# Cross attention in half chunks of 128 steps and groups of eight heads, with the queries in two slots

## The chip, the cores and the metric

The kernel runs on one core of a Trainium2 chip. The metric is the device time of one execution in microseconds (us); lower is better. Engines: PE is TensorE (matmul), PEld its weight loads, DVE VectorE, ACT ScalarE, POOL GpSimd, SP the queue that issues nearly all DMAs.

## What is computed

A two-layer decoder on x[2, 1024, 256] with a context of 77 rows. Layer 0 is self attention, cross attention and a mixture of eight linear experts; layer 1 is a tanh recurrence over the 1024 steps, cross attention and a gated mixture of experts. Each sublayer reads a layer norm of x and is added to x. Cut to what matters here:

```python
def xattn(x, y, wq, bq, wk, bk, wv, bv, wo, bo):       # 16 heads of 16, both layers
    scores = einsum('bhqd,bhkd->bhqk', q, k) / sqrt(D) # q from x, k and v from the 77 context rows
    out = einsum('bhqk,bhkd->bhqd', softmax(scores), v)
    return out @ wo + bo
def step(h, xt):                                       # layer 1, 1024 in a row
    h_new = tanh(xt + h @ Wh.T + bh)
x = x + attn0(ln(x)); x = x + xattn0(ln(x), ctx); x = x + ffn0(ln(x))
x = x + rnn1(ln(x));  x = x + xattn1(ln(x), ctx); x = x + ffn1(ln(x))
```

## The kernel before

Everything is one stage whose instructions are ordered at build time. `Plan` is a list scheduler: each kind of work (`st.add`) has an engine, a count, a cost in us, a rank, what it waits for, and whether it opens or closes one of five PSUM banks. The plan writes out a fixed order for each engine; at run time each engine follows its own order and waits on semaphores. Where PE would have nothing to do for over 0.1 us the plan puts filler matmuls there (`idle`, L549) whose results nobody reads.

The work goes by tiles of 128 steps of one batch. A **chunk** is four tiles (2 batches x 256 steps), eight halves of 128 steps in all. The recurrence (`Recurrence`) takes 12 small matmuls a step (L532, eight in `hi` and four in `lo`), two tanh (L575, L576) and a subtraction (L581); a step needs the one before it. Other work stands on PE between `hi` and `lo` and between steps. The recurrence starts once the first two tiles have been through all of layer 0, and after its last step the last two tiles still have to pass cross attention and the gated experts of layer 1.

Cross attention runs eight times by chunk (four in each layer), in the order that the list `order` gives. For each chunk: `Projection` makes the queries (L762, float32, two blocks), splits them into two float16 parts (ACT L789 to L793, DVE L800 to L805) and stores them in DRAM through SP (L823, L824, `xq_pair` to `qx_scr`). For each of four groups of four heads `load_q` (SP) writes rows of zeros into the row of maxima (L1248, two DMAs), and fetches the queries of both parities (L1252, two DMAs) into the one tile `x_qs`. `first_pass` (L1268) computes scores with queries as weights, `highest` (DVE L1280) takes the maxima, PE turns them (L1287), DVE keeps them (L1293), and SP writes them into that row of `x_qs` (L1301, two DMAs), so that the second pass of scores has them subtracted. The row has to hold zeros in the first pass, and the queries of a chunk may be loaded only when the scores of the chunk before are done (`s2`), as there is one `x_qs`. Then come `scores` (L1311, two matmuls of 256 columns into a bank, weights of 77 columns), `exp` (ACT L1322), `values` (L1336, four heads beside each other in the array, float32, 256 columns), and `Merge`: keep (L660), turn (L666), divide (L676, L683), turn (L691), output product (L714, L716), update of x (DVE L723). The update releases the next norm: L444 to L464, turned at L473.

Self attention (L983, L986, L1010, L1043, L1046, L1072, Merge with `tail` in place of `x_osb`) and the gated experts (L1708 make, L1739 spread, L1778 down) keep chunks of four tiles. Expert routing (`LinearExperts`, L1414 to L1465) also waits for all four tiles of its chunk.

## Time and profile before

| | |
|---|---|
| median of 3 runs | 1335.83 us (1330.74 to 1337.04) |
| profiled execution | 1334.48 us, of which the span is 1332.7 us |
| PE busy | 1290.1 us, 97% of the span |
| DVE, ACT busy | 858.2, 624.9 us |
| recurrence | first tanh at 196.1 us, last at 1214.0 us |

Busy time of PE overstates its load, since its matmuls overlap: the start-to-start distance of two matmuls in a row is shorter than the duration of one. The prediction therefore prices a matmul by the distance of starts.

### The profile page before, as it was taken

Reading aid. Unit: us, or ns where it says so; the run is one execution under the profiler, and the core shown is the slowest. Engines: PE = TensorE matmul, PEld = TensorE weight load, DVE = VectorE, ACT = ScalarE, POOL = GpSimd, SP = SyncE. Lnnn points to the kernel's source line nnn. Section 1 sums busy time; section 2 is a strip of 40 time slices with the busy share of each in tenths; the row PEclk is TensorE's granted clock in tenths of the full one; section 3 lists DMA queues with packets and bytes.
Section 4 is the critical chain, followed back from the end, with each engine's and each line's share of the span. In section 5 each row is a group of like instructions: output and inputs, shape, how many; then the busy total and the mean of one; then the engine's idle time right before and its main releaser. Section 6 shows DMA issues by size and latency. Waiting matters only on the chain.

```text
span 1332.7 us, 48565 instructions
## 1 busy us (share of the span) xinstructions
PE 1290.1 (97%) x19676; PEld 891.6 (67%) x19676; DVE 858.2 (64%) x2733; ACT 624.9 (47%) x2842; POOL 38.4 (3%) x60
## 2 busy tenths in 40 slices
PE   5798899999999999999999999999999999999998
PEld 3465447777767777766677778756777677766555
DVE  7876786387874249787822367776664845576486
ACT  2162415735336753643477766524443354343322
POOL 2000000000000000000000000000000000000000
PEclk9799999999999999999999999998997999999999
DMA  6543400010000001100000051000001000000100
GB/s 197 119 124 123 92 1 10 21 39 15 3 2 10 15 9 50 51 3 2 3 3 4 4 175 58 13 2 2 3 2 41 28 2 3 18 2 32 35 1 17
DMA packets 50753, 44.48 MB, mean 33 GB/s; under 512 B 10667, under 2 KB 49766, under 8 KB 50534
## 3 DMA queue, kind: packets, MB, share of 16 engines
q1 hardware_dynamic: 48934, 40.59, 10.2%
q8 instruction: 160, 2.62, 0.8%
q10 hardware_dynamic: 1600, 0.79, 0.3%
q14 instruction: 59, 0.48, 0.1%
HBM read 25.81 MB, written 15.15 MB: 31 GB/s over the span
## 4 chain that ended last, share of the span: by engine, by line
PE 92%; DVE 4%; DMA 2%; issue 1%; ACT 1%; SPq 0%; DVEq 0%; ACTq 0%
PE b L532 24%; PE b L1708 10%; PE b L1478 7%; PE b L1072 6%; PE b L549 6%; PE b L1043 5%; PE b L1778 5%; PE b L983 5%; PE b L714 3%; PE b L762 3%; PE b L1336 3%; PE b L1311 2%; PE b L63 2%; PE b L473 2%; PE b L666 2%; PE b L518 2%
## 5 line engine op out<-in xcount | busy, mean ns | idle before, releaser
L532 PEld LDWEIGHTS b<-hp,whp 128*128 128x128 f16 x12276 | 477.6, 96 | 252.3 <-ACT hp L575 164.3
L532 PE MATMUL b<-hp,whp 128*128 128x2 f16 x12276 | 535.4, 165 | 2.7 <-DVE hp L581 1.6
L575 ACT ACTIVATE hp<-b 128x4 f16<-128x4 f32 x1024 | 178.2, 174 | 442.9 <-PE b L532 432.4
L581 DVE TENSOR_TENSOR hp<-hist,hp 128x4 f16<-128x4 f32 x1023 | 164.4, 161 | 342.4 <-ACT hist L576 331.1
L992 DVE TENSOR_REDUCE mx<-b 128x1 f32<-128x512 f32 (+3 forms) x304 | 193.1, 655 | 4.9 <-PE b L986 2.9
L1057 ACT ACTIVATE vp<-b 128x512 f32<-128x512 f32 x288 | 170.7, 603 | 33.1 <-PE b L1046 19.7
L576 ACT ACTIVATE hist<-b 128x4 f32<-128x4 f32 x1024 | 179.3, 175 | 0.0
L1708 PE MATMUL b<-vp,heads 128*128 128x512 f16 x576 | 168.5, 385 | 0.0
L549 PE MATMUL b<-whp 128*128 128x512 f16 (+6 forms) x456 | 120.9, 335 | 0.0
L983 PE MATMUL b<-heads 128*128 128x512 f16 (+3 forms) x384 | 111.4, 333 | 5.8 <-DVE mx L992 3.8
L1478 PE MATMUL b<-we,xT 128*128 128x512 f16 x384 | 109.3, 377 | 0.0
L1043 PE MATMUL b<-heads 128*128 128x256 f16 (+1 forms) x640 | 104.8, 261 | 0.4
L1072 PE MATMUL b<-vp 128*32 128x256 f32 (+1 forms) x1280 | 95.2, 370 | 0.0
L1322 ACT ACTIVATE x_pr<-b 77x512 f32<-77x512 f32 x128 | 71.7, 593 | 28.5 <-PE b L1311 28.2
L1778 PE MATMUL b<-vp,heads 128*128 128x256 f16 x576 | 78.2, 272 | 0.0
L1504 DVE SCALAR_TENSOR_TENSOR x<-b,wts,x 128x256 f32<-128x256 f32 x128 | 61.7, 482 | 13.0 <-PE b L1478 9.4
L457 POOL TENSOR_TENSOR rs<-ve,neg_half 128x2 f32<-128x2 f32 x48 | 34.2, 712 | 1232.3 <-DVE ve L449 1232.1
L1043 PEld LDWEIGHTS b<-heads 128*128 128x128 f16 x640 | 53.5, 96 | 14.3 <-DVE mx L992 4.4
L1708 PEld LDWEIGHTS b<-vp,heads 128*128 128x128 f16 x576 | 48.2, 97 | 20.1 <-DVE x_nm L1280 0.4
L1280 DVE TENSOR_REDUCE x_nm<-b 128x4 f32<-128x308 f32 x128 | 56.7, 471 | 4.2 <-PE b L1268 3.4
L1778 PEld LDWEIGHTS b<-vp,heads 128*128 128x128 f16 x576 | 51.5, 97 | 9.9 <-DVE heads L1762 0.6
L983 PEld LDWEIGHTS b<-heads 128*128 128x128 f16 x384 | 36.7, 98 | 24.0 <-DVE mx L992 12.2
(234 smaller groups left out, 1592.6 us busy)
## 6 DMA issues: line engine op xcount, KB each, us to landing
x_qs<-qx_scr SPq DMA_DIRECT2D x64, 96.0 KB
qx_scr<-xq_pair SPq DMA_DIRECT2D x16, 256.0 KB, 2.1
heads<-q_scr SPq DMA_DIRECT2D x32, 96.0 KB
heads<-k_scr SPq DMA_DIRECT2D x12, 192.0 KB, 4.3
x<-in_x SPq DMA_DIRECT2D x8, 256.0 KB, 6.9
q_scr<-tail SPq DMA_DIRECT2D x8, 256.0 KB, 2.4
k_scr<-tail SPq DMA_DIRECT2D x8, 256.0 KB, 2.4
x_qs<-in_L_ffn_We SPq DMA_DIRECT2D x2, 1024.0 KB, 5.6
```

Source lines behind the costliest of these rows:

```text
L532: return pe.matmul(self.z(t)[:, m], self.w.whp[:, a, k, m * P:(m + 1) * P], self.g.hp16[:, (t - 1) % 2, part, k, :], start=False, stop=Tru ...
L549: pe.matmul(self.g.b7[:, 0:min(512, columns - at)], self.w.whp[:, 0, 0, 0:P], self.w.whp[:].rearrange("p a k n -> p (a k n)")[:, 0:min(512 ...
L575: act.activation(self.g.hp16[:, t % 2, 0], self.z(t), ACT.Tanh, scale=1 / LIFT).then_inc(self.s["hi_ready"], 1)
L576: act.activation(self.g.hist[:, :, :, t % (4 * HALF)], self.z(t), ACT.Tanh, scale=1 / LIFT).then_inc(self.s["full_ready"], 1)
L983: last = pe.matmul(o[:, at:at + P * n], self.qs[:, H // 2 * (h % 2) + h // 2, column(j):column(j) + P], self.ks[:, b, h // 2, P * first:P ...
L992: v.tensor_reduce(self.mx[:, column(j) // P, head:head + heads, int(first > 0)], self.st.bank("self_first", i)[:, 0:P * n * heads].rearran ...
L1043: last = pe.matmul(o[:, N * e:N * e + N], self.ks[:, b, h // 2, P * kb:P * kb + P], self.qs[:, H // 2 * (h % 2) + h // 2, QW * b + first:Q ...
L1057: act.activation(self.pr[:, n % 2, e0:e0 + heads, first:QW], self.st.bank("self_s", i)[:, 0:N * heads].rearrange("p (e n) -> p e n", e=hea ...
L1072: last = pe.matmul(o[QD * e:QD * e + QD, QW * b + first:QW * b + QW], self.va[:, b * (S // P) + kb, at:at + QD], self.pr[:, n % 2, e, firs ...
L1478: last = pe.matmul(o[:], x[:, k, column(j):column(j) + P], self.w.we[:, wt, k, D * e:D * e + 2 * D], start=at == 0, stop=at == self.PER - 1)
L1708: last = pe.matmul(o[:], wt[:, k, m * P:(m + 1) * P], x[:, k, :], start=at == 0, stop=at == 5)
L1778: last = pe.matmul(o[:, D * (p % 2):D * (p % 2) + D], self.hp[:, n % 3, h, P * p:P * p + P], wd[:, m, :], start=m == 0 and p % 2 == 0 and ...
```

## The change

Cross attention takes half chunks (`XT` = 2 tiles, `XW` = 256 columns) in two groups of eight heads (`XG` = 8, `NX` = 2). `x_qs` has the same size but two slots, so that the queries of a half may be loaded while those of the half before are in use. Only the first four groups write zeros. After that the row keeps the negated maxima of the group that used the slot before; the first pass then gives scores with those already subtracted, and `keep_max` adds the old row (kept in `x_mp`) to the new maxima. Scores take four matmuls of 128 columns into a bank in place of two of 256, values eight of 128 columns a unit in place of four of 256. `Merge`, the projection and the order of chunks follow; self attention keeps its sizes through parameters. The core of the diff, sizes that only follow left out:

```diff
+XT, XG = 2, 8
+XW, NX = XT * P, H // XG
...
     def divide(self, v, u):
-        if n and hg == 0:
-            v.wait_ge(self.s["turned"], TC * n)
+        if n >= self.ring and hg == 0:
+            v.wait_ge(self.s["turned"], T * (n - self.ring + 1))
...
     def make(self, pe, i):
-        pe.wait_ge(norm.s["stored"], TC * c + 3 + b)
+            pe.wait_ge(norm.s["stored"], self.T * (c + 1))
...
-        self.qs = st.sb(name + "_qs", [P, H // 2, CW], F16)
+        self.qs = st.sb(name + "_qs", [P, 2, H // 2, XW], F16)
...
+    def slot(self, g):
+        return self.qs[:, g // NX % 2]
...
     def load_q(self, sp, g):
-        if n:
-            sp.wait_ge(self.s["s2"], 2 * B * (g - NG + 1))
+        if n >= 2:
+            sp.wait_ge(self.s["s2"], 2 * B * (g - 2 * NX + 1))
+        else:
+            for p in range(2):
+                row = 64 * p + ROWS
+                sp.dma_start(self.slot(g)[row:row + 1, pairs, :],
+                             w.zero_row[:, 0:XW].unsqueeze(1).broadcast_to([1, XG // 2, XW])).then_inc(self.q_in[g % 2], 16)
+        self.proj.wait_kept(sp, n, range(KD * hg // NX, KD * (hg + 1) // NX))
         for p in range(2):
-            sp.dma_start(self.qs[row:row + 1, pairs, :], w.zero_row.unsqueeze(1).broadcast_to([1, HG // 2, CW])
...
     def keep_max(self, v, g):
+        if g < 2 * NX:
+            v.tensor_copy(self.mp[:, slot, :], src).then_inc(self.s["mp"], 1)
+        else:
+            v.wait_ge(self.m_in[g % 2], 32 * (g // 2 - NX + 1))
+            v.tensor_tensor(self.mp[:, slot, :], src, self.mp[:, slot, :], ALU.add).then_inc(self.s["mp"], 1)
...
     def load_max(self, sp, g):
+        sp.wait_ge(self.s["mp"], g + 1)
         if g >= 2:
-            v.wait_ge(self.m_in[g % 2], 32 * (g // 2))
+            sp.wait_ge(self.m_in[g % 2], 32 * (g // 2))
...
     def scores(self, pe, i):
-        for e in range(2):
-            h = HG * hg + 2 * (i % 2) + e
-            last = pe.matmul(o[0:M2, QW * e:QW * e + QW], ks[:, b, h, :], self.qs[:, h // 2, QW * b:QW * b + QW],
+        for e in range(HG):
+            h = XG * hg + HG * (i % 2) + e
+            last = pe.matmul(o[0:M2, P * e:P * e + P], ks[:, b, h, :], self.slot(g)[:, h // 2, P * b:P * b + P],
...
         order = [(0, 0), (0, 1), (0, 2), (1, 0), (0, 3), (1, 1), (1, 2), (1, 3)]
+        order = [(layer, 2 * c + i) for layer, c in order for i in range(2)]
```

What this makes of the order, at three places. **SP, layer 0, first chunk** (`xq_pair` to `qx_scr` stores queries, `x_ks` to `x_qs` the zeros, `x_mp` to `x_qs` the maxima). Before, from the first store of cross queries:

```order
L823 DMA qx_scr<-xq_pair 128x2x512
L824 DMA qx_scr<-xq_pair 128x512
L823 DMA qx_scr<-xq_pair 128x2x512
L824 DMA qx_scr<-xq_pair 128x512
L823 DMA q_scr<-tail 128x2x512
L824 DMA q_scr<-tail 128x512
L823 DMA k_scr<-tail 128x2x512
L824 DMA k_scr<-tail 128x512
L1248 DMA x_qs<-x_ks 1x2x512 x2
L1252 DMA x_qs<-qx_scr 48x2x512 x2
```

Now:

```order
L835 DMA qx_scr<-xq_pair 128x2x256
L836 DMA qx_scr<-xq_pair 128x256
L835 DMA q_scr<-tail 128x2x512
L836 DMA q_scr<-tail 128x512
L835 DMA qx_scr<-xq_pair 128x2x256
L836 DMA qx_scr<-xq_pair 128x256
L835 DMA q_scr<-tail 128x2x512
L836 DMA q_scr<-tail 128x512
L1269 DMA x_qs<-x_ks 1x4x256 x2
L1273 DMA x_qs<-qx_scr 48x4x256 x2
```

The first load now stands behind half as many stores of cross queries, and ahead of both stores of keys (`k_scr`), but still behind the second store to `q_scr`.

**PE, layer 0, first chunk**: L777 (now L788) is the projection of self attention's next chunk, L1268 (now L1288) the first pass. Before:

```order
L777 MATMUL b<-first,x_pr 128x512 x24
L63 MATMUL b<-x_pr,first 128x256 x12
L1268 MATMUL b<-x_ks,x_qs 128x154 x10
L1287 MATMUL b<-ident,x_nm 128x128
L1268 MATMUL b<-x_ks,x_qs 128x154 x6
```

Now:

```order
L788 MATMUL b<-first,x_pr 128x512 x13
L1288 MATMUL b<-x_ks,x_qs 128x154 x4
L788 MATMUL b<-first,x_pr 128x512 x3
L1288 MATMUL b<-x_ks,x_qs 128x154 x2
L788 MATMUL b<-first,x_pr 128x512
L1288 MATMUL b<-x_ks,x_qs 128x154 x2
L788 MATMUL b<-first,x_pr 128x512 x3
L1307 MATMUL b<-ident,x_nm 128x128
```

The first pass has moved ahead of eleven of the 24 projections and of the twelve L63, and stands among them.

**PE, after the last recurrence step, around the first pass of the last part** (L1778, now L1813, is the gated experts' down product, L549 the filler). Before:

```order
L549 MATMUL b<-whp 128x512 x3
L549 MATMUL b<-whp 128x448
L1268 MATMUL b<-first,x_qs 128x154 x6
L549 MATMUL b<-whp 128x256
L1268 MATMUL b<-first,x_qs 128x154 x2
L549 MATMUL b<-whp 128x512 x6
L549 MATMUL b<-whp 128x448
L1287 MATMUL b<-ident,x_nm 128x128
```

Now:

```order
L1288 MATMUL b<-first,x_qs 128x154 x6
L1813 MATMUL b<-vp,heads 128x256 x3
L1288 MATMUL b<-first,x_qs 128x154 x2
L1813 MATMUL b<-vp,heads 128x256 x3
L1288 MATMUL b<-first,x_qs 128x154 x2
L1813 MATMUL b<-vp,heads 128x256 x3
L1288 MATMUL b<-first,x_qs 128x154 x2
L1813 MATMUL b<-vp,heads 128x256 x3
L1307 MATMUL b<-ident,x_nm 128x128
```

Down products of the expert chunk before stand where filler stood.

## Rows read from the trace of the kernel before

**Rows 1.** The page: busy time by engine, share of the span, instructions.

```profile
PE 1290.1 (97%) x19676; PEld 891.6 (67%) x19676; DVE 858.2 (64%) x2733; ACT 624.9 (47%) x2842; POOL 38.4 (3%) x60
```

**Rows 2.** Busy time by stretch: stretch, length, each engine, clock, DMA.

```profile
98.50:196.00 97.50, 88.57 (x600) 48.41 (x599) 71.92 (x178) 32.03 (x68) 2.76 (x4) 0.98 0.28 74
196.00:1214.00 1018.00, 1015.02 (x17735) 728.86 (x17733) 631.48 (x2191) 520.56 (x2631) 22.47 (x32) 0.98 0.06 19
1214.00:1274.60 60.60, 60.51 (x424) 37.53 (x423) 35.18 (x84) 20.38 (x42) 2.43 (x3) 1.00 0.11 36
```

**Rows 3.** The tanh at L575: all, and those between 1018 and 1032 us.

```profile
L575 ACT ACTIVATE hp<-b x1024: 146/173/262, 196.1 to 1214.0; 128x4 f16<-128x4 f32 x171
...
1018.00:1032.00 14.00, 1.72 (x10) 0.51 0.13 45
```

**Rows 4.** Busy time of the filler L549 in two stretches (PE, then PEld).

```profile
196.00:1214.00 1018.00, 98.92 (x362) 26.81 (x362) 0.98 0.06 19
1214.00:1274.60 60.60, 18.13 (x78) 7.47 (x78) 1.00 0.11 36
```

**Rows 5.** Timeline of PE after the recurrence: start, duration, line, shape, count.

```profile
1232.09 2.75 PE L1708 MATMUL b<-vp,heads 128*128 128x512 f16 x12
...
1234.89 2.78 PE L1778 MATMUL b<-vp,heads 128*128 128x256 f16 x24
1237.51 0.27 PE L549 MATMUL b<-whp 128*128 128x256 f16 x1
```

**Rows 6.** Timeline of PE, cross attention of the first chunk.

```profile
121.41 0.30 PE L1268 MATMUL b<-x_ks,x_qs 128*128 128x154 f16 x2
...
135.49 0.80 PE L1311 MATMUL b<-x_qs,x_ks 128*77 128x256 f16 x4
```

**Rows 7.** Timeline of DVE: the last update by cross attention, first chunk and last.

```profile
156.62 0.39 DVE L723 TENSOR_TENSOR x<-b,x 128x256 f32<-128x256 f32 x1
...
1269.85 0.39 DVE L723 TENSOR_TENSOR x<-b,x 128x256 f32<-128x256 f32 x1
```

**Rows 8.** Timeline of SP: a group's zeros, queries, and maxima of two groups.

```profile
111.46 1.19 SPq L1248 DMA_DIRECT2D x_qs<-x_ks  x2
112.69 0.88 SPq L1252 DMA_DIRECT2D x_qs<-qx_scr  x2
...
135.07 3.27 SPq L1301 DMA_DIRECT2D x_qs<-x_mp  x4
```

**Rows 9.** Timeline of PE: short and long matmuls of the shapes that change.

```profile
83.88 0.43 PE L1072 MATMUL b<-vp 128*32 128x128 f32 x8
84.24 0.23 PE L1043 MATMUL b<-heads 128*128 128x128 f16 x1
84.31 0.22 PE L1046 MATMUL b<-mask_kq,identb 128*128 128x128 bf16 x1
84.36 0.22 PE L1043 MATMUL b<-heads 128*128 128x128 f16 x1
...
1253.13 0.63 PE L1311 MATMUL b<-x_qs,first 128*77 128x256 f16 x4
1253.69 0.64 PE L1336 MATMUL b<-x_pr,first 77*32 77x256 f32 x8
1254.26 0.33 PE L666 MATMUL b<-ident,x_osb 128*128 128x128 f32 x1
```

**Rows 10.** Weight loads: all of L1043 (page); timeline of PEld, two for scores.

```profile
L1043 PEld LDWEIGHTS b<-heads 128*128 128x128 f16 x640 | 53.5, 96 | 14.3 <-DVE mx L992 4.4
...
1253.13 0.15 PEld L1311 LDWEIGHTS b<-x_qs,first 128*77 128x77 f16 x2 [0.41 <-issue]
```

**Rows 11.** DMA issues of stored queries: size, us from issue to landing.

```profile
qx_scr<-xq_pair SPq DMA_DIRECT2D x16, 256.0 KB, 2.1
...
qx_scr<-xq_pair SPq DMA_DIRECT2D x16, 128.0 KB, 2.0
```

**Rows 12.** Timeline of PE: a stall inside the recurrence.

```profile
781.87 0.26 PE L532 MATMUL b<-hp,whp 128*128 128x2 f16 x4 [1.34 <-DVE hp L581]
```

More of the change, by code:

```diff
@@ L623, with __init__ @@
 class Merge:
-    def __init__(self, st, name, chunks, summed, rank, room):
+    def __init__(self, st, name, chunks, summed, rank, room, tiles, heads):
         self.st, self.g, self.name, self.chunks, self.summed = st, st.g, name, chunks, summed
@@ L738, in __init__ @@
         M, N = blocks, len(chunks)
-        self.per = 3 * KD if self.paired else B * KD
+        self.T, self.W = tiles, tiles * P
+        self.per = 3 * KD if self.paired else KD
         per = self.per
@@ L1094, in __init__ @@
         N = len(chunks)
[L1095 removed]
+        G = N * NX
         def block(n, m):
             w = chunks[n][1]
[L1099 to L1102 removed]
+            return w.wq[:, :, m * P:(m + 1) * P], None if w.bq is None else w.bq[:, m:m + 1], self.q_scr, m * P, XW * n, "query"
+        self.proj = Projection(st, name + "q", KD, xT, chunks, block, rank, room.pair, XT)
+        self.units = [(n, hg, b) for n in range(N) for hg in range(NX) for b in range(B)]
         early = lambda i: layers[i].early
@@ L1266, in first_pass @@
         for e in range(0, HG, 2):
-            h = HG * hg + e
-            last = pe.matmul(o[:, M2 * e:M2 * e + 2 * M2], self.qs[:, h // 2, column(j):column(j) + P],
+            h = XG * hg + HG * part + e
+            last = pe.matmul(o[:, M2 * e:M2 * e + 2 * M2], self.slot(g)[:, h // 2, P * b:P * b + P],
                              w.ks[:, b, h:h + 2, :], start=True, stop=True)
@@ L1315, in exp @@
     def exp(self, act, i):
-        u, e = i // 2, i % 2
+        u, part = i // 2, i % 2
         if i == 0 and self.guard:
@@ L1333, in values @@
         pe.wait_ge(self.s["vset"], B * (self.layers.index(w) + 1))
-        for e in range(HG):
-            at = VW * (HG * hg + e)
-            last = pe.matmul(o[QD * e:QD * e + QD, QW * b:QW * b + QW], w.vc[0:M2, b, at:at + QD],
-                             self.pr[0:M2, u % 2, e, :], start=True, stop=True, tile_position=(0, QD * e),
-                             skip_group_check=True)
+        for part in range(2):
+            for e in range(HG):
+                h = HG * part + e
+                at, col = VW * (XG * hg + h), QW * b + P * part
+                last = pe.matmul(o[QD * e:QD * e + QD, col:col + P], w.vc[0:M2, b, at:at + QD],
+                                 self.prob(u)[0:M2, h, :], start=True, stop=True, tile_position=(0, QD * e),
+                                 skip_group_check=True)
         last.then_inc(self.s["pv"], 1)
```

171 lines of the change are left out of this document (88 added, 83 removed).

## The prediction

> **What bounds the kernel now.** The page first: PE is busy 97% of the span, the next engine 64% [rows 1]. Busy shares are no load, so the view by stretch comes next. It gives three parts [rows 2]: before the recurrence (to 196 us), the recurrence (196 to 1214 us, 1018 us), and what follows it (119 us). The row of L575 gives the ends of the middle one [rows 3]: 1023 steps, 0.995 us each. In it PE is idle for 3 us of 1018, and filler is busy for only 99 us of them [rows 2, 4]. So the recurrence shares a full PE with everything else there, and a us of other PE work put into it costs a us. From 98.5 to 196 us PE sits idle for 8.9 us (97.5 less 88.57) [rows 2]: a chain of transfers and reductions. After the recurrence PE looks full, but filler is busy for 18.1 of 60.6 us [rows 4]; that filler stands for waiting too. What follows 1274.6 us, some 58 us of gated experts of the last chunk, has the same order in both kernels.
>
> So three sums are wanted: how much earlier the recurrence starts, what PE work and filler change inside it, and what changes behind it.
>
> **Prices** are distances of starts. Thirteen matmuls of 512 columns in float16 (twelve L1708 and one L1739) take 1232.09 to 1234.89: 0.215 us each; 24 of 256 take 1234.89 to 1237.51: 0.109 [rows 5]. One of 128 columns takes 0.055 (84.31 to 84.36) [rows 9]. Four score matmuls of 256 columns take 0.56 us with the start of the run [rows 9], 0.109 each when they run on. Values of four heads, eight records, take 0.57 us with 256 columns (1253.69 to 1254.26) and 0.36 with 128 (83.88 to 84.24) [rows 9]. So 128 columns more cost 0.21, and 0.15 is paid on leaving this kind of matmul.
>
> **Scores.** 256 matmuls of 256 columns become 512 of 128. At 0.056 that is 28.7 us for 27.9: +0.8. No row shows weights of 77 columns behind so short a matmul. The lower bound is that 0.056. The upper is the whole weight load, about 0.115 (0.15 us for two, the second starting 0.03 to 0.04 behind the first) [rows 10]: 512 x 0.115 less 27.9 = +31. I take 0.056, since the second load starts after 0.034 us, which fits behind 0.053 us of columns, and the L1043 matmuls run at 0.055 though their own loads last 0.096 [rows 10].
>
> The Trainium skill (TensorE: Matmul & The Clock Gate, LDWEIGHTS and Weight-path perf modes) speaks against this. It has a load take its columns over 1.2 GHz, and the fast load only with 128 weights that aren't float32: 64 ns for these 77, more than the 56 of the matmul. By it the scores would cost 4.1 us more; the row with two loads 0.034 apart does not agree.
>
> **Values.** 64 units, each now two runs of four heads with 128 columns. If the second run follows without a break a unit costs 0.36 + 0.21 = 0.57 as before; if the 0.15 is paid twice, 64 x 0.15 = +9.3. I take zero, as the 0.15 belongs to the change of kind, and keep +9 for the range.
>
> **Before the recurrence.** Cross attention of the first chunk lasts from the first pass at 121.4 to the last update, which ends at 157.0 [rows 6, 7], with scores only from 135.5 [rows 6]. In the new order the first pass stands 11 projections and 12 L63 earlier: 11 x 0.215 + 12 x 0.109 = 3.7 us, so 117.7. What PE must do from there to the first scores is these 3.7, eight L1268 more, and turns: about 123, and the maxima of the first group (up to 1.6 us of issue [rows 8], two of transfer, taken from the stores [rows 11]) are in by about 123.5. The queue does not stop that. The four groups cost 2.07 us of issue each [rows 8] in either kernel, as all four still write zeros; halved stores land no sooner (2.0 us for 128 KB, 2.1 for 256) [rows 11]; but the maxima of the first group now stand behind the first three loads only. From 123.5 the PE work that is placed up to the last output product is 27 to 28 us: last update about 152, 5 us earlier. Behind it two tiles' norms remain where there were four (the other two are done during the second half): 3 us. The routing of experts is as before. Moved out of this part are 5 first passes of self attention, 10 score matmuls, two runs of values and their masks: 3.2 us of PE, which makes room. So **-8 us**. Bounds: -3.2 if only the moved work counts, -12 if all 8.9 us of idle time go too.
>
> **In the recurrence.** Counted in the two orders: the 3.2 us of self attention come in. Of cross attention come in 16 first passes (1.1), four float32 projection products (1.7), scores 192 of 256 columns to 416 of 128 (20.9 to 23.3: 2.4), values 48 to 50 units (1.1), turns (0.7): 7.0. Gated experts move out behind it: 24 makes, 24 downs and a spread: -8.0. Filler goes from 144,512 to 147,648 columns, +1.3 at 0.215 for 512. Sum **+3.5**. DVE and ACT get 32 splits of 256 columns for 16 of 512; with 62% and 51% busy [rows 2] they hide a fixed part of about 0.2 us each. SP loses 56 zero DMAs at 0.6 us [rows 8]: covered, worth nothing by itself. New waits: `load_max` waits for the maxima two groups before, with the next query loads and expert output stores behind it in SP; one that follows at once waits under a us, and PE's next scores follow over two us behind. `keep_max` waits for a transfer four groups back: long done.
>
> **Behind it.** The 8.0 of experts come in. Out go 1.1 (first pass), 1.7 (projection), 1.7 (scores), 1.1 (values), 0.7 (turns): 6.3, as only one half remains whole. Filler falls from 43,328 to 18,880 columns: -10.2. Sum **-8.5**. Does the chain allow it? Before, the last update ends 56 us after the last tanh (1270.2) [rows 3, 7]. Now there are two groups to load without zeros (1.8 us of issue for 8.3), eight exponentials for 16, two tiles of output products for four. Going through the new order with these prices I get it at 44 us, and PE work with filler of 50 us before the common last part, which began at 60.4: room for a few us of waits.
>
> **Sum**: -8 + 3.5 - 8.5 = -13, on 1334.48: 1321.5. The profiled execution lies 1.35 below the median, so the forecast is **1323 us**.
>
> **Rivals.**
> *Filler stood for waits that halves don't shorten* (same). The columns of filler are the plan's guess at waits; where it takes a transfer as done too early, PE waits as long as before. Then the tail gives +1.7 rather than -8.5, and I get 1333. For it: latency does not fall with size [rows 11]. Against it: down products now stand in the gaps, and 8.3 us of issue really go. 0.18.
> *Weight loads of scores bind at 64 ns.* In this kernel: 512 scores 0.008 us dearer, 1327. This is the skill's price above. Against it stands [rows 10]. 0.08.
> *The recurrence stalls* (slower). PE is in order: if a group's scores or first pass stand before their maxima or queries have landed, the recurrence stops with them, and now 14 halves pass there with two exchanges each. A stall of that kind shows once, 1.3 us before L532 at 781.9 [rows 12], where it waited for DVE behind other work. It cancels the gain at 13/26 = 0.5 us for each of the 26 groups; at 0.9 to 1.2 each I get 1348. Against it: before shows nearly no idle PE in the recurrence, and loads may now start a half earlier. 0.12.
> *More is gained.* All idle time before the recurrence goes (4 us more). Also the clock: between 1018 and 1032 it was at 0.51 of full speed, 1.2 GHz, and ten tanh ran in 14 us where 14 would have [rows 3]; before the fall PE had mostly recurrence steps. A mean of 0.98 over the recurrence [rows 2] makes 30 to 50 us at that level; less or more of it moves the time by up to 15 us either way. With the idle time and half of that I get 1311. 0.14.
> That the change does not do what it says (halves do not overlap) is the first rival.
>
> **How the numbers follow.** Forecast 0.48, own range 1316 to 1329. A measurement of this kernel tells about 0.5%, 6.7 us, so faster is below 1329.2 and slower above 1342.5. Faster: nearly all of the forecast, most of the 64 ns, the better case: 0.66. Same: 0.22. Slower: 0.12. The range reaches to 1308 for the better case with the clock, and to 1340 for the first rival, values at +9 and a small stall.
>
> **What would show it.** First tanh near 188 us (wrong: 193 or later). The 1023 steps in 1018 to 1026 us (over 1035: stalls; idle PE in that stretch names them, and scores by their distance of starts: 0.056, or 0.064, or 0.1). Last tanh to end about 110 us, filler there about 8 us less, last update by cross attention 42 to 47 us behind the last tanh. A unit of values at 0.57 us, or 0.72. The share of half clock, as it can hide the rest.

## The result and the profile after

The change made the kernel slower by half a per cent: median 1341.9 us (1338.8 to 1345.0, 8 runs) where the kernel before has 1335.5 (1328.5 to 1337.3, 8 runs); the ratio is 1.0051, 95% interval 1.0034 to 1.0069. Forecast was 1323, range 1308 to 1340. The profiled execution of after took 1339.26 us, its span is 1337.5. One execution of a variant (12) took 1801.7 us at a mean granted clock of 0.584; it is left out of every figure below.

Busy time of after by engine, from the page; it answers to [rows 1] and says as little as that did:

```profile
PE 1288.6 (96%) x20400; PEld 912.5 (68%) x20400; DVE 859.2 (64%) x2749; ACT 628.3 (47%) x2858; POOL 38.4 (3%) x60
```

Busy time by stretch of after (stretch, length, PE, PEld, DVE, ACT, POOL, granted clock, DMA share, GB/s), and the tanh, now L577. They answer to [rows 2] and [rows 3]:

```profile
98.50:196.10 97.60, 87.17 (x653) 50.93 (x651) 69.09 (x173) 29.30 (x67) 2.75 (x4) 0.93 0.28 74
196.10:1228.60 1032.50, 1026.12 (x18408) 751.65 (x18410) 635.51 (x2214) 528.96 (x2655) 22.87 (x32) 0.98 0.07 20
1228.60:1337.50 108.90, 104.28 (x761) 65.07 (x756) 76.24 (x162) 33.52 (x64) 2.06 (x3) 1.00 0.06 18
...
L577 ACT ACTIVATE hp<-b x1024: 146/173/262, 196.1 to 1228.6; 128x4 f16<-128x4 f32 x171
```

The first tanh comes at 196.1 as before, where 188 was forecast. The recurrence takes 1032.5 us for 1017.9, where +3.5 was forecast. What follows takes 108.9 us for 118.7, where -8.5 was forecast. So one of three sums held. In the profiles the forecast misses by 17.8 us (1339.26 for 1321.5): 8 ahead of the recurrence, 11.1 in it, less 1.3 behind it.

Filler, now L551, in the recurrence and up to the last part (PE, then PEld), for [rows 4]; and the last update by cross attention (L733, on DVE), for [rows 7]:

```profile
196.10:1228.60 1032.50, 101.02 (x371) 27.58 (x371) 0.98 0.07 20
1228.60:1279.20 50.60, 5.67 (x25) 2.41 (x25) 1.00 0.09 28
...
1274.58 0.39 DVE L733 TENSOR_TENSOR x<-b,x 128x256 f32<-128x256 f32 x1
```

Scores (L1340) and values (L1371) of after, timeline of PE, for [rows 9]:

```profile
147.18 0.64 PE L1371 MATMUL b<-x_pr,x_vc 77*32 77x128 f32 x16
147.76 0.64 PE L1340 MATMUL b<-x_qs,x_ks 128*77 128x128 f16 x8
148.33 0.64 PE L1371 MATMUL b<-x_pr,x_vc 77*32 77x128 f32 x16
```

A unit of values takes 0.58 us from its start to the next start. The eight scores shown take 0.57, 0.071 each with the start of the run; over all 27 runs of eight the median is 0.457, 0.057 each. Both prices of the forecast hold.

**Where the rest went** stands in the granted clock. Stretches at 1.2 GHz in the recurrence, before (busy time by stretch):

```profile
359.40:362.80 3.40, 3.40 (x50) 2.35 (x47) 3.04 (x11) 0.73 (x6) 0.00 (x0) 0.50 0.02 5
912.40:919.20 6.80, 6.80 (x58) 4.73 (x55) 3.73 (x19) 1.77 (x9) 0.00 (x0) 0.50 0.01 2
1018.20:1031.90 13.70, 13.70 (x144) 9.38 (x142) 3.62 (x17) 3.25 (x23) 0.00 (x0) 0.50 0.14 46
1165.00:1171.80 6.80, 6.70 (x79) 3.60 (x78) 3.62 (x14) 2.32 (x14) 0.00 (x0) 0.50 0.01 2
```

The same in after, with one ahead of the recurrence first:

```profile
126.10:136.40 10.30, 8.59 (x74) 5.68 (x75) 6.33 (x15) 3.98 (x8) 0.00 (x0) 0.50 0.27 78
784.90:802.00 17.10, 14.42 (x147) 10.38 (x146) 6.76 (x23) 5.87 (x24) 0.69 (x1) 0.50 0.42 129
880.50:890.70 10.20, 10.20 (x159) 7.56 (x157) 4.52 (x21) 4.98 (x23) 0.00 (x0) 0.50 0.01 2
935.10:948.70 13.60, 13.60 (x197) 10.73 (x196) 5.40 (x28) 6.29 (x29) 0.00 (x0) 0.50 0.01 2
1177.40:1184.20 6.80, 6.80 (x49) 3.92 (x49) 3.61 (x17) 1.67 (x10) 0.00 (x0) 0.50 0.12 37
```

To turn this into time I took every matmul's distance to the next start, and from it the median distance of the same pair of kinds at full clock in the same trace. Summed over a half-clock stretch this is what it lost; one excess above 0.25 us outside such a stretch, or above 1 us in it, counts as a stall. The rest is work, filler and short waits. In us:

| profiled execution | first tanh | recurrence | half clock | lost in it | stalls | rest | last tanh to end |
|---|---|---|---|---|---|---|---|
| before | 196.1 | 1017.9 | 30.7 | 12.1 | 2.5 | 1003.3 | 118.7 |
| after | 196.1 | 1032.5 | 47.8 | 19.3 | 5.8 | 1007.5 | 108.9 |

The rest grows by 4.2, where 3.5 was counted. Half clock adds 7.2 and stalls 3.3.

**Every execution says the same.** Each comes with its time and its mean granted clock; twice what is missing to 1, times the span, is its time at half clock. The executions of before range from 1345.8 us on average at 0.969 (3 of them) over 1335.9 at 0.979 (23) to 1328.2 at 0.986 (2). Over 208 executions of 14 kernels of this study, each kernel about its own mean, a us at half clock goes with 0.36 us of time (correlation 0.96; 0.24 to 0.43 within single kernels). That gives each kernel an estimate of its time with its half clock taken off: before 1315.8, after 1312.0. It is a straight line carried on to no half clock, which no execution had. After is the shorter one by 3.8 us, and has 84 us of half clock in the median where before has 56: 28 x 0.36 = 10 us lost. In sum +6.

**The stall.** PE, then ACT, in after near 787 us:

```profile
784.16 0.25 PE L534 MATMUL b<-hp,whp 128*128 128x2 f16 x4 [1.20 <-DVE hp L583]
...
785.91 1.20 PE L773 MATMUL b<-xT,x_wq 128*128 128x256 f32 x2
789.79 0.37 PE L534 MATMUL b<-hp,whp 128*128 128x2 f16 x8 [2.68 <-ACT hp L577]
...
789.28 0.38 ACT L802 ACTIVATE xq_pair<-b 128x256 f16<-128x256 f32 x1 [4.59 <-DMA qx_scr<-xq_pair]
789.56 0.17 ACT L577 ACTIVATE hp<-b 128x4 f16<-128x4 f32 x1
```

and the DMA issues between 770 and 800 us (KB each, us to landing), beside [rows 11]:

```profile
heads<-in_down SPq DMA_DIRECT2D x1, 1536.0 KB, 7.3
tail<-in_gate SPq DMA_DIRECT2D x1, 1536.0 KB, 11.8
...
qx_scr<-xq_pair SPq DMA_DIRECT2D x4, 128.0 KB, 5.0
```

L802 splits a block of projected queries into one of two slots, and waited 4.6 us for the store that frees it. That store had been issued behind the two weight loads and landed with them: its two DMAs, issued at 777.7 and 778.4, landed at 787.4 and 789.2, the second weight load at 788.7. (The 5.0 of the last line is the median of two such late ones and two prompt ones.) The fall of the clock at 784.9 lies ahead of this stall, behind the one of 1.2 us. ACT is in order, so the tanh waited behind L802, and the recurrence with it. In before the same stores were issued at 786.7, after the weights had landed; with halves the first queries of the second layer are ready 9 us earlier. Nothing in the forecast had looked at what stands in the DMA queue ahead of a store that moves.

### The profile page after: what moved, and what is told of

It is laid out like the page before. It is cut to its first block, busy times and chain, and to the rows that moved or that the text cites. A ratio compares the mean times of both kernels' runs of the same rounds, so it can differ in the third digit from the quotient of the medians.

```text
span 1337.5 us, 50092 instructions
## 1 busy us (share of the span) xinstructions
PE 1288.6 (96%) x20400; PEld 912.5 (68%) x20400; DVE 859.2 (64%) x2749; ACT 628.3 (47%) x2858; POOL 38.4 (3%) x60
## 4 chain that ended last, share of the span: by engine, by line
PE 91%; DVE 4%; DMA 1%; issue 1%; ACT 1%; SPq 1%; DVEq 0%; ACTq 0%
PE b L534 23%; PE b L1743 10%; PE b L1513 7%; PE b L1084 6%; PE b L551 6%; PE b L1055 5%; PE b L1813 5%; PE b L995 4%; PE b L724 4%; PE b L1371 3%; PE b L1340 2%; PE b L773 2%; PE b L671 2%; DVE mx L1004 2%; PE b L475 2%; PE b L63 2%
## 5 line engine op out<-in xcount | busy, mean ns | idle before, releaser
L577 ACT ACTIVATE hp<-b 128x4 f16<-128x4 f32 x1024 | 177.4, 173 | 435.7 <-PE b L534 425.3
L1743 PE MATMUL b<-vp,heads 128*128 128x512 f16 x576 | 165.1, 382 | 0.0
L551 PE MATMUL b<-whp 128*128 128x512 f16 (+7 forms) x412 | 110.6, 336 | 0.0
L1813 PE MATMUL b<-vp,heads 128*128 128x256 f16 x576 | 78.9, 272 | 0.1
L1351 ACT ACTIVATE x_pr<-b 77x512 f32<-77x512 f32 x128 | 72.4, 593 | 13.7 <-PE b L1340 13.4
L1813 PEld LDWEIGHTS b<-vp,heads 128*128 128x128 f16 x576 | 51.5, 97 | 9.9 <-DVE heads L1797 0.6
```

The source lines that it names most:

```text
L551: pe.matmul(self.g.b7[:, 0:min(512, columns - at)], self.w.whp[:, 0, 0, 0:P], self.w.whp[:].rearrange("p a k n -> p (a k n)")[:, 0:min(512 ...
L577: act.activation(self.g.hp16[:, t % 2, 0], self.z(t), ACT.Tanh, scale=1 / LIFT).then_inc(self.s["hi_ready"], 1)
L1743: last = pe.matmul(o[:], wt[:, k, m * P:(m + 1) * P], x[:, k, :], start=at == 0, stop=at == 5)
L1813: last = pe.matmul(o[:, D * (p % 2):D * (p % 2) + D], self.hp[:, n % 3, h, P * p:P * p + P], wd[:, m, :], start=m == 0 and p % 2 == 0 and ...
```

## Experiments

The theory was that the counts are right, and that a stall and the half clock, which depend on the order that the planner makes, hide them. The rivals were dearer work, a chain ahead of the recurrence, and half clock that comes with the halves themselves. Line numbers of the variants are shifted by 5 to 15 where lines were added.

**1. Weight loads behind the stores.** After, with rows of two queues moved and PE's order unchanged:

```diff
+MOVED = [("sp", [("load_second", 2), ("load_whole", 0)], ("x_load_q", 15)),
+         ("v", [("router", 0), ("router", 1)], ("n5_stats", 6))]
```

> Kernel after, with two rows of SP moved: the loads of the gated experts' weights (L2064 to L2078) stand behind the projected queries' stores of the next two halves instead of ahead of them, and DVE's two rows that split the router weights stand after the next norm. The order of PE is unchanged. Theory (a stall, and then the clock): in after, ACT waited 4.6 us at 789.3 for a store of queries that had been queued behind 3 MB of weights, PE stood still for 3.1 us, and the granted clock fell to 1.2 GHz from 784.9 to 802.0. If the stall brings the clock down, both go: 4 to 5 us of waits and some 5 us of slow matmuls, so about 1332 us where after has 1341.9, ratio to before about 0.998, and no more than 7 us at half clock between 780 and 805. Rival (the float32 query products there bring the clock down by themselves, whatever waits): the wait goes, the half clock of 14 to 17 us stays, ratio about 1.002.

Measured: 1344.0, ratio 1.0071 (1.0046 to 1.0095). The 4.6 us wait is gone, and a worse one came, of ACT for the weights at their split. Two stretches, and that wait:

```profile
784.80:795.50 10.70, 7.43 (x117) 5.95 (x116) 4.37 (x18) 3.01 (x17) 0.69 (x1) 1.00 0.65 196
795.80:809.40 13.60, 6.25 (x77) 3.97 (x78) 5.24 (x13) 4.84 (x17) 0.00 (x0) 0.50 0.47 162
...
802.19 0.84 ACT L2099 ACTIVATE heads<-tail 128x768 f16<-128x768 f32 x1 [11.27 <-DMA tail<-in_gate]
```

The total missed both the 1332 of the theory and the rival's. But the clock answered: it was full over ten of the same float32 products (L773, here L778), which the rival had blamed, and fell within the stall of 11 us, which began at 792.0.

**2. Filler at three places of half clock.** After, with

```diff
+FILLED = [(662, 677, 256), (714, 731, 256), (961, 976, 256)]
...
+            if name == "hi":
+                added += [("idle", columns) for low, high, columns in FILLED if low <= i < high]
```

> Kernel after, with one filler matmul of 256 columns behind the first products of 47 steps of the recurrence, in three places: steps 662 to 676, 714 to 730 and 961 to 975. These are the stretches that came before, and lay in, the half clock of 880.5 to 890.7, 935.1 to 948.7 and 1177.4 to 1184.2. Nothing else is moved. Cost by the price of 0.109 each: 5.1 us. Theory (the clock falls where PE streams few columns, and this is what after loses against the forecast): these three stretches, 30.7 us long with 13.3 us lost in them, stay at full clock, so -8 us: ratio to before about 0.999. Rival (the falls come from something else than the columns that PE streams there): the half clock stays as it is or only moves, and the time rises by the 5 us of filler: ratio about 1.009.

Measured: 1334.7, ratio 0.9996 (0.9966 to 1.0026), 7.2 us less than after, as the theory had it. The profile, from step 662 or so on:

```profile
900.00:1020.00 120.00, 119.95 (x2017) 85.94 (x2014) 80.53 (x273) 51.02 (x286) 3.44 (x5) 1.00 0.01 3
1020.00:1100.00 80.00, 79.58 (x1326) 59.53 (x1324) 47.19 (x174) 36.09 (x196) 0.69 (x1) 0.87 0.10 29
1100.00:1228.30 128.30, 127.75 (x2289) 92.64 (x2291) 78.94 (x271) 58.20 (x327) 2.07 (x3) 1.00 0.04 13
```

All three places are at full clock (the first lies at 872 to 888 here, and between 801.5 and 1040.4 this trace has no half clock); two new stretches came between 1020 and 1100, where there was no filler. Over the executions half clock fell from 84 to 57 us and the time without it rose by 3.1: a filler of 256 columns cost 0.07 here, not 0.109, since some stood in waits.

**3. Filler around the first scores.** After, with 36 matmuls of 128 columns:

```diff
+EARLY = {(name, i): 4 for name, i in [("x_first", 4), ("x_first", 5), ("x_first", 6), ("x_first", 7),
+         ("x_turn_max", 1), ("x_scores", 0), ("x_scores", 1), ("x_scores", 2), ("x_scores", 3)]}
```

> Kernel after, with 36 short filler matmuls (128 columns, 0.055 us each, 2.0 us in all) between the first passes and the first scores of the first cross attention, where PE waited for 3 us between 122 and 128 and the clock then fell to half for 10.2 us. Nothing else is moved. Theory (the start did not come earlier because of the clock): that half-clock stretch goes or shrinks to 3.4 us, the last update of the first cross attention ends near 154 instead of 158, and the first tanh comes at 191 to 193 instead of 196.1; the whole about 4 us shorter, ratio to before about 1.002. Rival (the transfers set the start and the clock falls in any case): half clock from 126 as before, first tanh at 196 to 198, ratio 1.005 to 1.007.

Measured: 1336.6, ratio 1.0012 (0.9984 to 1.0041), 5.3 us less than after. The half clock at 126 was gone, but the first tanh came only at 194.9, 1.2 us earlier, where the theory had 191 to 193, with the filler's own 2 us on the way to it and a stretch of half clock left at 161.7. The first pass itself came 1.1 us later than in after (118.8 for 117.7), with 20.5 us of half clock ahead of 98.5 us where after has 13.7, so from the first pass to the end of the last update 2.3 us were gained (37.7 for 40.0). Over the executions half clock fell from 84 to 69 us, 5.4 us by the 0.36. This left the start open (13).

**4. Zeros back.** Load and add-back as before, halves and slots as after:

```diff
             sp.wait_ge(self.s["s2"], 2 * B * (g - 2 * NX + 1))
-        else:
-            for p in range(2):
+        for p in range(2):
...
-            v.tensor_tensor(self.mp[:, slot, :], src, self.mp[:, slot, :], ALU.add).then_inc(self.s["mp"], 1)
+        v.tensor_copy(self.mp[:, slot, :], src).then_inc(self.s["mp"], 1)
```

> One part of the change undone: the queries' rows for the maxima are again written with zeros before each group (two more DMAs on SP for each of the 28 later groups) and the maxima are copied, not added to the old ones. Halves, groups of eight heads and two slots stay. Theory (the zeros are covered in the recurrence and worth little in it; in the last part they cost issue time ahead of the queries): first tanh unchanged at 196, time from the last tanh to the end 0 to 3 us longer than the 108.9 of after, total 0 to 4 us longer than after, besides what the clock does. Rival (the removed zeros made the gain of the last part): the last part goes back to 115 us or more and the total is 6 to 8 us longer than after. Third: the add-back with its two new waits was itself what made the recurrence longer; then 3 us or more shorter than after.

Measured: 1330.4, ratio 0.9965 (0.9936 to 0.9994). It is 11.5 us less than after. The first tanh stayed at 196.2. The first two expectations missed the total; the third, 3 us or more shorter, has it, but not by its reason: without half clock (8.1 us lost) and stalls (4.8) the recurrence takes 1013.0 us, 5.5 more than in after. The recurrence and what follows:

```profile
196.20:1222.00 1025.80, 1020.11 (x18464) 750.18 (x18463) 638.37 (x2220) 530.74 (x2657) 23.13 (x32) 0.99 0.07 20
1222.00:1329.20 107.20, 102.58 (x719) 63.45 (x718) 72.94 (x156) 31.99 (x61) 2.07 (x3) 0.99 0.06 18
```

The last part is 107.2 us, not longer: the issue time of zeros that the forecast took out there shows nothing beyond the 107.1 to 108.9 us of after's three orders (10 to 12). The costs that the planner assumes had changed its order, and half clock fell from 84 to 52 us in the median. With half clock taken off it stands at 1312.7, after at 1312.0. So no gain of the part that was undone shows; since other orders of after lie up to 8 us from it by this measure, a few us either way are not excluded.

**5. Short reductions.** After, with 23 reductions of self attention's first pass cut to 128 columns, so that part of these maxima is left out:

```diff
+        width = P if 39 <= i < 62 else P * n * heads
```

> Kernel after, with the 23 reductions of self attention's first pass (L1004, items 39 to 61) that DVE has between the last update of the first cross attention and the first linear expert product cut to 128 columns (so the maxima of these tiles are left out in part). The order of every engine is the same. In after DVE was busy for 16.6 of 17 us there, 12.9 of them with these reductions, and the 13 small steps of the routing of experts (L1449 to L1475, 164.1 to 173.4) stood between them. Theory (DVE sets this stretch, which is why fewer first passes on PE bought nothing): the reductions fall from 540 and 672 ns to about 200, the routing ends 6 to 8 us earlier, and the first tanh comes at 188 to 191 instead of 196.1. Rival (the chain of norms, router products and transfers sets it, or the clock): the first tanh stays at 195 to 196.

One execution: first tanh 195.7. DVE was busy for 11.4 us of 17 instead of 16.6, the routing's last step came 1.8 us earlier, and PE, in order, got to the product behind it 0.4 us earlier. Counted from the end of the last update, which came 0.5 us later here, the first tanh is 0.9 us earlier (37.5 for 38.3), not the 5 to 8 of the theory. The rival holds: DVE's reductions did not set that stretch. (1345.2 us, clock 0.966.)

**6. Weight loads later still.** As 1, with the loads near 855 us and the splits on ACT and DVE at steps 664 to 701.

> Kernel after, with the loads of the gated experts' weights moved to a place where SP has nothing behind them for 12 us (behind the projected queries' loads of group 23, near 855 us), and their splits on ACT and DVE moved with them (to steps 664 to 701, before the first use at step 716). PE's order is unchanged. The run before showed the clock at full speed from 784 to 795 with the same float32 products once the 4.6 us wait was gone, but its loads then held up ACT at their split for 11 us. Theory (stall, then clock): no PE stall over 1 us between 775 and 870, at most 7 us of half clock between 780 and 870, recurrence 8 to 10 us shorter than the 1032.5 of after, ratio to before about 0.998 to 0.999 in the median. Rival (the clock falls there all the same, or the splits in their new place take from the recurrence what was won): half clock of 10 us or more in 780 to 870 or behind 870, ratio 1.003 to 1.006.

Measured: 1337.7, ratio 1.0006 (0.9981 to 1.0031), 4.2 us less than after; without half clock 1311.6. The place of the stall and what follows:

```profile
770.00:870.00 100.00, 99.72 (x1844) 82.77 (x1841) 61.69 (x243) 51.40 (x258) 5.50 (x8) 1.00 0.24 74
871.40:885.10 13.70, 13.54 (x205) 9.65 (x198) 8.61 (x29) 6.92 (x28) 0.00 (x0) 0.50 0.33 118
```

The stall and its 17 us of half clock are gone, yet the recurrence takes 1031.8 us, where the theory had 8 to 10 less than 1032.5, and the time without half clock is 0.4 us less than after's; the fall that stood at 880 came 9 us earlier and 3 us longer, and the splits cost nine small stalls of 0.25 to 1 us. The theory was right for the place of the stall, the rival for what lies behind it.

**7. Filler in the kernel before.** As 2, at the four places of before, 56 steps.

> The kernel before, with one filler matmul of 256 columns behind the first products of 56 steps of the recurrence (158 to 167, 708 to 722, 812 to 828, 964 to 977), the four places in which its own trace showed half clock. Cost 56 x 0.109 = 6.1 us against 12.1 us lost there. Theory (the clock is a cost of the arrangement, in before as in after): half clock in the recurrence falls from 30.7 us to 10 or less, 3 to 6 us faster than before, ratio 0.996 to 0.998. Rival (before's clock losses were not of this kind, and filler helps only after): ratio 1.002 to 1.005.

Measured: 1335.1, ratio 1.0005 (0.9974 to 1.0037). Three of four places are at full clock, a new one came at 786 (behind the stall of [rows 12], 1.7 us here). In the recurrence of the profile 23.9 us of half clock are left, where the theory had 10 or less. Over the executions half clock fell from 56 to 40 us, worth 5.8; the time without it rose by 4.2, 0.075 for each filler. In before too filler raised the clock, without the gain of the theory: it bought about what it cost.

**8 and 9. Another order of the same kernel.** After, with one number of the planner changed:

```diff
-        st.add("act", name + "_exp", self.exp, 2 * len(self.units), 0.52, lambda i: of_unit(i // 2) + 0.31,
+        st.add("act", name + "_exp", self.exp, 2 * len(self.units), 0.54, lambda i: of_unit(i // 2) + 0.31,
```

> Kernel after with a single number of the planner changed, the cost that it assumes for an exponential of cross attention, 0.52 to 0.54 us. The same instructions are issued, in an order that differs in many places. It shows how much of the difference between before and after is the accident of one order. Theory (half clock and stalls depend on the order, not on the halves): the part of the recurrence that is neither half clock nor a stall stays within 3 us of the 1007.5 of after, while what the half clock takes moves by several us from 19.3. Rival (halves bring the half clock with them): it stays at 17 to 22 us.

One execution: 1326.7. Recurrence 1022.2, lost by half clock 12.5, stalls 1.5, rest 1008.2.

> The order of the run before (kernel after, assumed cost of a cross attention exponential 0.54 instead of 0.52), now timed against the kernel before. Theory (what after lost was the half clock and the stall of its own order; its count of work is what was forecast): recurrence without half clock and stalls 1007 to 1009 us, no PE stall of 3 us near 785, total 1326 to 1331, ratio 0.992 to 0.997. Rival (the one look was a lucky execution): ratio 1.002 or more.

Measured: 1322.1, ratio 0.9918 (0.9889 to 0.9947), 4 us below the range of the theory. In its profile 17.1 us of the recurrence are at half clock (7.2 lost), where the same kernel in 8 had 30.7: two executions of one order differ too. The tanh:

```profile
L577 ACT ACTIVATE hp<-b x1024: 147/174/258, 194.5 to 1212.4; 128x4 f16<-128x4 f32 x171
```

**10 to 12. Three orders of each kernel.** The same number at 0.50, and at both values in before.

> Kernel after, the same planner number at 0.50: another order of the same instructions. Theory (order decides the half clock): recurrence without half clock and stalls again 1005 to 1011 us; half clock and stalls together anywhere from 10 to 28 us; total 1325 to 1343. Rival (halves bring the losses with them): half clock and stalls 22 us or more in the recurrence, ratio 1.003 or more.

> Kernel before with the same planner number at 0.54. Theory (order decides): the part of the recurrence without half clock and stalls stays at 1001 to 1006 us, the time from the last tanh to the end at 116 to 121, and half clock and stalls scatter by several us about the 14.6 of before: total 1329 to 1343. Rival (before is steady, only after scatters): within 2 us of before.

> Kernel before with the planner number at 0.50, a second other order. The same expectation as for 0.54; with it there are three orders of each kernel. If the forecast's count is right and only the orders' half clock hid it, the three of after are, half clock and stalls taken off, 4 to 10 us shorter in sum than the three of before.

| kernel, number | median | ratio (95%) | half clock, median | without half clock | rest of the recurrence |
|---|---|---|---|---|---|
| before, 0.52 | 1335.5 | 1 | 56 | 1315.8 | 1003.3 |
| before, 0.54 | 1339.7 | 1.0040 (1.0018 to 1.0063) | 58 | 1318.1 | 1000.5 |
| before, 0.50 | 1338.5 | 1.0020 (0.9992 to 1.0049) | 75 | 1312.1 | 994.6 |
| after, 0.52 | 1341.9 | 1.0051 (1.0034 to 1.0069) | 84 | 1312.0 | 1007.5 |
| after, 0.54 | 1322.1 | 0.9918 (0.9889 to 0.9947) | 54 | 1303.6 | 1009.4 |
| after, 0.50 | 1333.9 | 0.9983 (0.9952 to 1.0013) | 67 | 1310.2 | 1011.7 |

(Lost in half clock and stalls, in the profiles' recurrences: 18.9 and 12.6 for before at 0.54 and 0.50, 8.5 and 19.7 for after. The rest missed its range by up to 0.7 us for three of these orders, and by 6 for before at 0.50, which moved work from the recurrence to both sides of it: first tanh 204.3, last part 124.1.) Half clock lies at 56 to 75 in the orders of before and 54 to 84 in those of after: it depends on the order, and three of each show no more of it with halves. Without it the means are 1315.3 and 1308.6, 6.7 us apart. Single orders scatter about these means by 3.0 and 4.4 us (standard deviation), so the 6.7 have a standard error of 3.1: three orders of each make a gain likely and don't show its size. 20 us lie between the fastest and the slowest order of after, 4 between those of before.

**13. The start at full clock.** The order at 0.54 with filler as in 3, and 32 more matmuls of 128 columns around the norms behind the last update.

> The order of kernel after with the planner number at 0.54, and short filler matmuls on PE ahead of the recurrence, where its profile showed half clock at 127.3 to 137.6 and 161.4 to 168.3 (10.9 us lost in the two): 36 of 128 columns around the first scores and 32 around the norms behind the last update, most of them in waits of PE. It asks where the 8 us went that the forecast saw ahead of the recurrence. Theory (half clock took the larger part of them): both stretches stay at full clock, the first tanh comes at 187 to 190 instead of 194.5, total 3 to 6 us shorter, ratio 0.988 to 0.990. Rival (the first cross attention and the routing behind it are a chain that the clock hardly touches): the first tanh stays at 192.5 or later, total within 2 us.

Measured: 1322.4, ratio 0.9912 (0.9883 to 0.9941). The stretch ahead of the recurrence, the tanh, and the last update of the first cross attention:

```profile
98.50:190.70 92.20, 84.45 (x695) 50.44 (x694) 66.35 (x166) 28.64 (x64) 2.75 (x4) 1.00 0.30 78
...
L592 ACT ACTIVATE hp<-b x1024: 147/174/258, 190.7 to 1218.6; 128x4 f16<-128x4 f32 x171
...
153.27 0.42 DVE L748 TENSOR_TENSOR x<-b,x 128x256 f32<-128x256 f32 x1 [0.36 <-PE b L739]
```

At full clock the first tanh comes at 190.7, 3.8 us earlier than in 9 and just outside the 187 to 190 of the theory, and the last update ends at 153.7 (after: 157.7; forecast: 152). Of the 10.9 us that the expectation counts as lost there, full clock gave back 3.8. The total did not follow, as the rival had it: in the profile, the slowest of the five executions, half clock in the recurrence was 47.8 us where 9 had 17.1. But over the executions half clock was less than in 9, 45 us for 54, and the time without it 3 us more (1306.6 for 1303.6). Where these 3 us come from is not shown.

**14. All filler.** With 32 matmuls of 256 columns in the recurrence besides.

> The run beside it with 32 more filler matmuls of 256 columns in the recurrence (steps 714 to 725, 824 to 833, 958 to 969), at the three places where that order had 17.1 us of half clock and 7.2 us lost. Cost: 2.6 us by what such filler cost in the runs so far (0.08 each). Theory (filler pays where half clock is): half clock in the recurrence under 7 us, 2 to 5 us shorter than the run without. Rival (the falls move to other sparse stretches, as they did from 784 to 871 and from 912 to 786 in the runs so far): within 2 us, half clock 14 to 20 us as before.

Measured: 1320.7, ratio 0.9902 (0.9874 to 0.9930), on 4 runs. Half clock in the recurrence was 20.5 us in the profile, as the rival said, and it stands at the three places of 9, not at others: at 926.3, right behind the first group of filler, at 1021.8 and at 1158.4, with the filler running. Filler (L566) in these last two stretches:

```profile
1021.80:1032.10 10.30, 2.97 (x8) 0.88 (x8) 0.50 0.01 2
1158.40:1165.20 6.80, 1.97 (x5) 0.46 (x5) 0.50 0.04 12
```

So filler of this size did not keep the clock up here. The executions had 29 us of half clock in all in the median, against 45 in 13. This is the fastest kernel of the study, and not to be told from 9.

**15. Stalls alone.** Before, with ACT copying 256 columns four, eight and twelve times behind the tanh of steps 300, 440 and 660.

```diff
+HELD = {300: 4, 440: 8, 660: 12}
...
+            if name == "tanh" and i in HELD:
+                rows.append(("hold", HELD[i]))
```

> The kernel before, with ACT held up behind the tanh of three steps in dense stretches of full clock: four copies of 256 columns behind step 300, eight behind 440, twelve behind 660 (some 1.7, 3.5 and 5 us each). Nothing else is changed. PE has to stand still there, and nothing sparse stands around it. It measures what a stall costs besides itself. Theory (a stall of 3 us or more brings the clock down by itself): no fall at step 300, a fall to 1.2 GHz within 4 us of the stall at 440 and at 660, 3 to 7 us long each, with 1 to 2.5 us lost in each besides the stall. Rival (only thin work brings it down): full clock at all three.

One execution. What PE waited, and the clock behind the second and the third:

```profile
496.77 0.35 PE L539 MATMUL b<-hp,whp 128*128 128x2 f16 x8 [0.36 <-ACT hp L582]
...
644.60 0.52 PE L539 MATMUL b<-hp,whp 128*128 128x2 f16 x12 [2.25 <-ACT hp L582]
...
869.53 0.38 PE L539 MATMUL b<-hp,whp 128*128 128x2 f16 x8 [4.60 <-ACT hp L582]
...
646.80:650.20 3.40, 3.40 (x43) 2.10 (x44) 2.57 (x9) 0.53 (x5) 0.00 (x0) 0.50 0.03 6
...
868.70:875.50 6.80, 5.97 (x92) 5.27 (x93) 5.00 (x20) 4.11 (x17) 0.00 (x0) 0.50 0.01 3
```

As the theory said: no fall with 0.36 us, one with 2.25 and with 4.60 (there within the stall), in stretches that are at full clock without them. Set beside the same steps of before, the tanh fall behind by 2.4 us at the second stall and by 1.2 more up to step 448, and by 4.7 at the third and 1.4 more up to step 668. So a stall cost itself and 1.2 to 1.4 us more where it stood. Not in sum: this recurrence had 23.9 us of half clock where that of before had 30.7, as the 13.7 us of before at 1018 did not come.

## Why the prediction was wrong

**The step that failed is the clock**, put at nothing in the sum; with it 3 us of stalls and the start, below. It stood in the forecast as "less or more of it moves the time by up to 15 us either way", beside the sum and not in it, and had a chance only in the better case. The trace held what was needed to price it: 30.7 us of half clock in the recurrence, and tanh rows in [rows 3] that show what it takes. What could not be read from it is where another order puts its half clock. That PE had "mostly recurrence steps" before the fall at 1018 is loose: from 1010 on, filler and expert products of up to 512 columns stood between the steps. In the profiles after got 17 us more of it in the recurrence and 3 us more ahead of it (27.3 for 23.9); by its executions, 28 us more in all, 10 us of time. The faster side was given 0.66 on a sum of 13 us, while one planner number alone moves the kernel before by 3 to 4 us and after by 8 to 20.

**Prices of scores and values**: right. 0.057 each and 0.58 a unit. The rival of 64 ns for the weight load of scores is gone: 27 runs of eight took 0.457 us in the median, which is 0.057 each and leaves no room for it. The Trainium skill (TensorE: Matmul & The Clock Gate, LDWEIGHTS) gives the load by its columns over 1.2 GHz, 64 ns for 77; the measurement differs, and decides.

**Ahead of the recurrence, -8**: 0 in the profile, and some of that is chance. The first tanh of before came later in the two other profiles that have its order up to there (7 and 15):

```profile
L590 ACT ACTIVATE hp<-b x1024: 146/173/262, 199.0 to 1218.8; 128x4 f16<-128x4 f32 x171
...
L582 ACT ACTIVATE hp<-b x1024: 147/174/257, 199.6 to 1220.9; 128x4 f16<-128x4 f32 x171
```

With the 196.1 that makes 198.2 in the mean, where four profiles of after's order (after, 1, 2, 6) have 196.1 to 197.5, 196.7 in the mean: by these the start came 1.5 us earlier. The first pass stood where it was forecast (117.7), but the first scores came at 126.3, not 123.5, and at 125.9 at full clock (13), so that much is no matter of the clock: the sum had counted PE's work between them and not the waits of 0.3 to 0.6 us, five of them and 2.3 us in all, that stand on PE between 122 and 126.3. From the first scores to the end of the last update, 28.5 us in the forecast, it took 31.4 in after, with half clock until 136.4, and 27.8 at full clock (13, another order). There the last update ends at 153.7 against the forecast 152, and the first tanh is 5.4 us earlier than in the profile of before; 3.8 of these came with the full clock (against 9), the rest with the order. Of the last 2.7 us, 1.7 lie ahead of the update and 1.0 behind it, 37.0 us to the first tanh instead of 36, with filler of up to 3.7 us in both. Which wait sets the part behind the update stays open: the reductions (5) do not.

**In the recurrence, +3.5**: +4.2 without half clock and stalls in the two profiles, with them +14.6. That 4.2 is so near is in part luck: over three orders of each the same rest is 10 us longer in after (1009.5 for 999.5), 7.6 without before at 0.50, which had moved work out of the recurrence.

**The rival of stalls** was right in sign, wrong in mechanism. Groups did not wait for maxima or queries at 26 places; one stall of 2.7 us came from a slot that waited for a store behind 3 MB of weights, and it followed one of 1.2 that before has too [rows 12]. That SP was "covered" looked at issue times, not at what a DMA stands behind. Seen from [rows 12] alone, where DVE was late at the same moment, the place was marked.

**Behind it, -8.5**: -9.8, right, and in all orders (107.1 to 108.9 us for 118.7 to 124.1). The last update ends 46.4 us behind the last tanh (42 to 47 forecast), filler there fell by 12.5 us (8 forecast). Of the reasons given, the queries' issue without zeros has no part that shows: with zeros back (4) it is no longer.

**Sum**: without half clock, after is 3.8 us shorter than before in its own order, 12.2 in the order at 0.54, which has no such stall, and 6.7 (standard error 3.1) in the mean of three orders. That the order at 0.54 measures 1322.1, so near the forecast 1323, is luck: it is the best of three, and had the half clock of before (54 us for 56) by its order alone.

## What to carry over

When a change makes a scheduler issue everything in a new order, price the granted clock as a term of its own, with its scatter, before trusting a sum of 1%; a few variants of one irrelevant planner number, in both kernels, show how large that scatter is. Compare kernels at equal clock: time over clock of single executions was nearly a straight line here, and its distance between two kernels is what their two orders are worth without the clock; what the code is worth takes several orders of each. Where a store or load moves, look at what is queued ahead of it, as an engine that waits for its slot may hold the critical loop.

## What the hardware showed

A us at half clock went with 0.36 us here, and 0.40 in the recurrences of the two profiles (12.1 of 30.7, 19.3 of 47.8). The Trainium skill (TensorE: Matmul & The Clock Gate, Terms) takes the penalty as half of the throttled time, 0.5; the runs show less. The tanh on ACT took 0.17 us at either level [rows 3]. That ACT, DVE and the latency between engines make up the rest is argued, not shown.

PE's clock fell to 1.2 GHz during or behind a stall of 2.25 us or more each time that there was one at full clock (1, 2, 3, 5, 15). Near 785 most kernels have a smaller one: where its excess was 1.3 to 1.8 us the clock fell behind it in five profiles of eight (after, 4, 7, 10, 11; not in before, 12 and 15), where it was 0.5 to 1.1 us it did not (8, 9, 13, 14). In after the fall at 784.9 stands behind the stall of 1.2 us and ahead of that of 2.7. The clock also fell with PE busy throughout, in stretches of recurrence steps, scores, values and router products, as at 880.5 and 935.1. Filler of 256 columns a step went with full clock in six of the seven places of 2 and 7, and the clock then fell elsewhere; in 14, at three more, the clock fell at each all the same. What brings the clock down there stays open.
